# A latent-attention layer on one core: the split of the attention scores goes from fp32r to fp16

## What is computed

```python
q_c = hidden_size @ Wq_c.T + bq_c                               # 192 wide
q = (q_c @ Wq_up.T + bq_up).reshape(b, s, NH, Q_HEAD)            # 128 + 64 per head
kv = hidden_size @ Wkv_c.T + bkv_c                               # 64 + 64 wide
k = concatenate([k_nope, k_rope]); v = ...                       # both from kv
scores = einsum('bhqd,bhkd->bhqk', q, k) / sqrt(Q_HEAD)
attn = softmax(scores, axis=-1)
o = einsum('bhqk,bhkv->bhqv', attn, v)
out = einsum('bhsv,Hv->bsH', o, Wo) + bo                         # heads are summed
```

## Time and profile before

| | |
|---|---|
| median of 3 runs (lowest to highest) | 1978.44 us (1977.9 to 1979.36) |
| the profiled execution, its own time | 1978.39 us |
| its span (first to last instruction) | 1976.4 us |
| mean granted TensorE clock | 0.992 of full speed |
| prepare, attention, feed_forward and what surrounds it | 0 to 93, 93 to 1830, 1830 to 1976 us of the span |
| busy share of the span: PE, PEld, DVE, ACT, POOL | 98%, 73%, 82%, 68%, 56% |

### The profile page before, as it was taken

The page is one execution under the profiler, slowest core; times in us unless marked ns, Lnnn a source line. Parts: engine busy times, 40 slices in busy tenths (PEclk is TensorE's granted clock), DMA queues, the critical chain, the costliest instruction groups (busy, mean ns, idle before and its releaser), DMA issues. The chain is left out here.

```text
span 1976.4 us, 37173 instructions
## 1 busy us (share of the span) xinstructions
PE 1937.1 (98%) x11014; PEld 1441.7 (73%) x11014; DVE 1622.0 (82%) x2585; ACT 1353.8 (68%) x2488; POOL 1102.3 (56%) x1215
## 2 busy tenths in 40 slices
PE   7999999999999999999999999999999999999798
PEld 6767777777777777777777777777777777777576
DVE  6588888888888888888888888888888888888665
ACT  4367777777777777777777777777777777777443
POOL 3336566565665665655656656656656566565710
PEclk9899999999999999999999999999999999999899
DMA  5521111111111111111111111111111111111211
GB/s 201 194 62 32 43 40 34 43 34 41 44 33 43 40 35 43 36 39 43 34 42 43 32 43 40 35 43 36 40 43 32 43 39 35 43 34 33 75 43 43
DMA packets 74308, 95.19 MB, mean 48 GB/s; under 512 B 25856, under 2 KB 48416, under 8 KB 74272
## 3 DMA queue, kind: packets, MB, share of 16 engines
q1 hardware_dynamic: 70176, 86.33, 17.1%
q0 software_dynamic: 4096, 8.40, 1.2%
HBM read 83.95 MB, written 10.75 MB: 48 GB/s over the span
## 5 line engine op out<-in xcount | busy, mean ns | idle before, releaser
L832 DVE TENSOR_TENSOR PTL<-X,PTH 128x512 f16<-128x512 f32 x1024 | 658.6, 685 | 147.8 <-ACT PTH L783 142.0
L783 ACT ACTIVATE PTH<-X 128x512 f16<-128x512 f32 x1024 | 554.3, 594 | 281.5 <-PE X L692 281.5
L848 DVE TENSOR_REDUCE mx<-S 128x1 f32<-128x1024 f32 x512 | 623.6, 1218 | 3.0 <-PE S L712 3.0
L798 ACT ACTIVATE prob<-S,shift 128x1024 f32<-128x1024 f32 x512 | 574.2, 1121 | 1.7 <-DVE shift L856 1.6
L692 PEld LDWEIGHTS X<-ident,prob 128*128 128x128 f32 x4096 | 469.2, 141 | 120.6 <-issue 53.3
L692 PE MATMUL X<-ident,prob 128*128 128x128 f32 x4096 | 538.1, 274 | 5.3 <-ACT prob L798 5.3
L710 PE MATMUL S<-kvTH,qeH 128*128 128x512 f32 x1024 | 445.5, 435 | 1.6 <-DVE qeL L837 1.6
L712 PE MATMUL S<-kvTH,qeL 128*128 128x512 f32 x1024 | 406.0, 396 | 0.0
L711 PE MATMUL S<-kvTL,qeH 128*128 128x512 f32 x1024 | 401.9, 392 | 0.0
L658 POOL TENSOR_TENSOR onormH<-osum,recip_row 128x512 fp32r<-128x512 f32 x128 | 198.5, 1551 | 288.7 <-ACT osum L806 288.7
L643 POOL TENSOR_TENSOR wvH<-wv,unit_tile 128x128 fp32r<-128x128 f32 x128 | 57.4, 448 | 393.4 <-PE V L763 387.7
(11 more groups left out here) (202 smaller groups left out, 1972.2 us busy)
## 6 DMA issues: line engine op xcount, KB each, us to landing
recip_row<-row_scratch SPq DMA_DIRECT2D x128, 256.0 KB, 4.2
weff<-weff_scratch SPq DMA_DIRECT2D x128, 192.0 KB, 4.0
wv<-in_wv POOLq DMA_DIRECT2D x128, 64.0 KB, 3.7
raw<-in_raw SPq DMA_DIRECT2D x8, 772.0 KB, 5.2
weff_scratch<-w_split SPq DMA_DIRECT2D x8, 768.0 KB, 4.8
x<-in_x SPq DMA_DIRECT2D x4, 1024.0 KB, 6.8
x_all<-in_x SPq DMA_DIRECT2D x3, 1024.0 KB, 6.8
out<-y SPq DMA_DIRECT2D x3, 1024.0 KB, 4.2
```

The source lines that it names most:

```text
L783: nc.scalar.activation(PTH[p][:, part:part + 4, unit * P:(unit + 1) * P], X[:, k % 2, :].rearrange("p (k c) -> p k c", k=4), ACT.Copy).the ...
L798: nc.scalar.activation(prob[u][:], S[:, u % 2, :], ACT.Exp, bias=shift[:, col:col + 1], accum_out=rs[:, col:col + 1]).then_inc(probs_ready, 1)
L832: v.tensor_tensor(PTL[p][at], X[:, k % 2, :].rearrange("p (k c) -> p k c", k=4), PTH[p][at], ALU.subtract).then_inc(low_out, 1)
L848: v.reduce_max(mx[:, col:col + 1], S[:, u % 2, :], AX.X).then_inc(max_ready, 1)
```

## The change

The scores are computed from fp16 halves in place of fp32r ones. fp16 has a narrow range of exponents, so both sides are scaled by powers of two: the key latents by `scale` (per latent, from the bound that also scales the values) while ACT reads them, and the projected queries by `qscale`, from a bound on what a query can reach; the exponential multiplies the scores by `unscale`.

In attention: kvTH, kvTL, qeH, qeL are fp16. ACT reads O twice, to qef (fp32) and to qeH (fp16), each with bias and scale tiles; POOL subtracts them to qeL at the end of its step, and DVE's `low_q` is gone. PE waits for q_high, not q_low, before it uses O again. The exponential takes a scale tile. DVE makes the shift with two dependent instructions on 128x1, not one.

In prepare: DVE takes two maxima of absolute values per group of heads; ACT takes absolute values of all latent weights, not of the key ones alone; PE adds eight one-column matmuls in the last turn and three small ones near the end, two of which wait for DVE's steps; DVE adds `reach_of_queries` ahead of wcAH and `scale_of_queries` in place of one instruction (L484). The matmul with `diag` becomes a transpose.

The diff, without declarations of tiles and semaphores and the renamed lines of the key bound:

```diff
             def turn_back(n):
 
-                pe.wait_ge(diag_ready, 1)
                 for u in range(UN):
-                    last = mm(psN[:, u * KVL:(u + 1) * KVL], kvf[0:KVL, u * P:(u + 1) * P], diag[:], start=True, stop=True)
+                    last = nc.tensor.transpose(psN[:, u * KVL:(u + 1) * KVL], kvf[0:KVL, u * P:(u + 1) * P], ident[0:KVL, 0:KVL])
                 last.then_inc(n_done, 1)
 
             def turn(n, nxt):
                 if nxt is None:
                     project(n, (0,))
+                    pe.wait_ge(wabs_ready, 3)
+                    for c in (1, 2):
+                        for k in range(KT):
+                            last = mm(psT[0][:, c - 1:c], wabs[:, k, c * P:(c + 1) * P], ones[:], start=(k == 0),
+                                      stop=(k == KT - 1))
+                    last.then_inc(qbound_done, 1)
...
                 mm(out, wcBHL[:], keep["qbL"][:, tok], start=False, stop=True).then_inc(cT_done, 1)
+                if n == 1:
+                    pe.wait_ge(q_step, REACH)
+                    pe.wait_ge(n_out, NB + 1)
+                    mm(psN[:, B0 + 1:B0 + 2], ones_all[:], reach[:, 0:1], start=True, stop=True).then_inc(reach_done, 1)
+                if n == 2:
+                    pe.wait_ge(q_step, TERM)
+                    pe.wait_ge(proj_out, 3 * NB)
+                    mm(psB[0:1, 0:P], term[:], ident[:], start=True, stop=True).then_inc(term_turned, 1)
+            pe.wait_ge(q_step, TOP)
+            mm(psN[:, B0 + 2:B0 + 3], ones_all[0:1, :], top[0:1, :], start=True, stop=True).then_inc(top_spread, 1)
...
-                for half in range(2):
-                    nc.scalar.activation(wabs[:, :, half * KVL:(half + 1) * KVL], wl[:, :, 0:KVL],
-                                         ACT.Abs).then_inc(wabs_ready, 1)
-                nc.scalar.activation(pbabs[:], pb[:, 3:4], ACT.Abs).then_inc(wabs_ready, 1)
+                nc.scalar.activation(wabs[:, :, 0:P], wl[:, :, 0:P], ACT.Abs).then_inc(wabs_ready, 1)
+                nc.scalar.activation(pbabs[:], pb[:], ACT.Abs).then_inc(wabs_ready, 1)
                 read_turned(n, range(UN))
+                nc.scalar.activation(wabs[:, :, P:3 * P], wl[:, :, P:3 * P], ACT.Abs).then_inc(wabs_ready, 1)
...
+                    if j == 0:
+                        act.wait_ge(k_scaled, 1)
+                    factor, bias = (scale[:, 0:1], kbias[:, 0:1]) if j == 0 else (1.0, pb[:, j:j + 1])
+                    nc.scalar.activation(out[:], src[:], ACT.Identity, bias=bias, scale=factor)
+                    nc.scalar.activation(keep[hi][:, tok], src[:], ACT.Identity, bias=bias, scale=factor).then_inc(proj_out, 1)
...
                 high, low = split[i][:, :, 0, :], split[i][:, :, 1, :]
+                v.reduce_max(wmax[:, ds(g, 1), 0], full[:, :, 0, :], AX.XY, apply_absolute_value=True)
+                v.reduce_max(wmax[0:QB, ds(g, 1), 1], full[0:QB, :, 1, :], AX.XY, apply_absolute_value=True)
...
                 dve.wait_ge(scale_out, 1)
                 v.tensor_scalar(scale[:], scale[:], 2.0 ** 14, None, ALU.mult).then_inc(scale_out, 1)
                 dve.wait_ge(scale_out, 2)
-                v.tensor_scalar(diag[:], ident[0:KVL, 0:KVL], scale[0:KVL, 0:1], None, ALU.mult).then_inc(diag_ready, 1)
+                v.tensor_scalar(kbias[:], pb[:, 0:1], scale[:, 0:1], None, ALU.mult).then_inc(k_scaled, 1)
+
+            def reach_of_queries():
+
+                dve.wait_ge(qbound_done, 1)
+                v.scalar_tensor_tensor(out=bound[:, 1:3], in0=psT[0][:, 0:2], scalar=NORM_MAX, in1=pbabs[:, 1:3],
+                                       op0=ALU.mult, op1=ALU.add).then_inc(q_step, 1)
+                dve.wait_ge(split_done, groups + 1)
+                v.reduce_max(wtop[:], wmax[:].rearrange("p g s -> p s g"), AX.X).then_inc(q_step, 1)
+                dve.wait_ge(q_step, 2)
+                v.tensor_tensor(reach[:, 1:2], wtop[:, 1:2], bound[:, 2:3], ALU.mult).then_inc(scale_out, 1)
+                dve.wait_ge(scale_out, 3)
+                v.scalar_tensor_tensor(out=reach[:, 0:1], in0=wtop[:, 0:1], scalar=bound[:, 1:2], in1=reach[:, 1:2],
+                                       op0=ALU.mult, op1=ALU.add).then_inc(q_step, 1)
+
+            def scale_of_queries():
+
+
+                dve.wait_ge(bias_in, 16)
+                v.tensor_scalar(keep["beff"][KVL:P, :], bqr[KVL:P, :], SCALE, None, ALU.mult).then_inc(q_step, 1)
+                dve.wait_ge(q_step, 4)
+                v.reduce_max(btop[:], keep["beff"][:], AX.X, apply_absolute_value=True).then_inc(q_step, 1)
+                dve.wait_ge(q_step, 5)
+                dve.wait_ge(reach_done, 1)
+                v.scalar_tensor_tensor(out=term[:], in0=psN[:, B0 + 1:B0 + 2], scalar=btop[:, 0:1], in1=kinv[:],
+                                       op0=ALU.add, op1=ALU.mult).then_inc(q_step, 1)
+                dve.wait_ge(term_turned, 1)
+                v.reduce_max(top[0:1, :], psB[0:1, 0:P], AX.X).then_inc(q_step, 1)
+                dve.wait_ge(top_spread, 1)
+                v.tensor_scalar(qpower[:], psN[:, B0 + 2:B0 + 3], TINY, None, ALU.max).then_inc(q_step, 1)
+                dve.wait_ge(q_step, 8)
+                v.tensor_scalar(qpower[:].bitcast(I32), qpower[:].bitcast(I32), 0x7F800000, None,
+                                ALU.bitwise_and).then_inc(q_step, 1)
+                dve.wait_ge(q_step, 9)
+                v.tensor_scalar(keep["unscale"][:], qpower[:], 2.0 ** -14, None, ALU.mult).then_inc(q_step, 1)
+                dve.wait_ge(q_step, 10)
+                v.reciprocal(qpower[:], keep["unscale"][:]).then_inc(q_step, 1)
+                dve.wait_ge(q_step, 11)
+                v.tensor_tensor(keep["qscale"][:], qpower[:], kinv[:], ALU.mult).then_inc(q_step, 1)
+                dve.wait_ge(q_step, 12)
+                v.tensor_scalar(keep["beff"][:], keep["beff"][:], keep["qscale"][:, 0:1], None, ALU.mult)
...
+                    reach_of_queries()
...
-        qeH = [sb(f"qeH{i}", [P, BLK], F32R) for i in range(2)]
-        qeL = [sb(f"qeL{i}", [P, BLK], F32R) for i in range(2)]
+        qef = [sb(f"qef{i}", [P, BLK]) for i in range(2)]
+        qeH = [sb(f"qeH{i}", [P, BLK], F16) for i in range(2)]
+        qeL = [sb(f"qeL{i}", [P, BLK], F16) for i in range(2)]
...
+
+            def low_q(nxt, i):
+                pool.wait_ge(q_high, nxt + 1)
+                nc.gpsimd.tensor_tensor(qeL[i][:], qef[i][:], qeH[i][:], ALU.subtract).then_inc(q_low, 1)
+
+            low_q(0, 0)
...
+                if exists(g) and exists(g + 1):
+                    if not isinstance(g, int) or g >= 1:
+                        pool.wait_ge(wv_split, g)
+                    low_q(g + 1, 1 - par)
...
                         if exists(g + 1) and on:
-                            pe.wait_ge(q_low, g + 2)
+                            pe.wait_ge(q_high, g + 2)
...
-                nc.scalar.activation(qeH[i][:], O[:], ACT.Identity, bias=keep["beff"][:, ds(h, 1)]).then_inc(q_high, 1)
+                bias, factor = keep["beff"][:, ds(h, 1)], keep["qscale"][:, 0:1]
+                nc.scalar.activation(qef[i][:], O[:], ACT.Identity, bias=bias, scale=factor)
+                nc.scalar.activation(qeH[i][:], O[:], ACT.Identity, bias=bias, scale=factor).then_inc(q_high, 1)
...
                     nc.scalar.activation(prob[u][:], S[:, u % 2, :], ACT.Exp, bias=shift[:, col:col + 1],
+                                         scale=keep["unscale"][:, 0:1],
...
-            def low_q(nxt, h, i):
-                dve.wait_ge(q_high, nxt + 1)
-                v.scalar_tensor_tensor(out=qeL[i][:], in0=O[:], scalar=keep["beff"][:, ds(h, 1)],
-                                       in1=f32(qeH[i][:]), op0=ALU.add, op1=ALU.subtract).then_inc(q_low, 1)
-
-            low_q(0, 0, 0)
...
-                    v.scalar_tensor_tensor(out=shift[:, col:col + 1], in0=mx[:, col:col + 1], scalar=bias, in1=lifted,
-                                           op0=ALU.add, op1=ALU.subtract, reverse1=True).then_inc(shift_ready, 1)
+                    v.scalar_tensor_tensor(out=top[:, col:col + 1], in0=mx[:, col:col + 1], scalar=keep["unscale"][:, 0:1],
+                                           in1=bias, op0=ALU.mult, op1=ALU.add).then_inc(top_ready, 1)
+                    dve.wait_ge(top_ready, 4 * g + u + 1)
+                    v.tensor_tensor(shift[:, col:col + 1], lifted, top[:, col:col + 1], ALU.subtract).then_inc(shift_ready, 1)
...
-                    if u == 1 and on and exists(g + 1):
-                        low_q(g + 1, h + 1 if not isinstance(g, int) else (h + 1) % NH, 1 - par)
...
-                "inv": sb(inner, "kv_inv", [P, 1]),
-                "kvTH": sb(inner, "kvTH", [P, TOK], F32R), "kvTL": sb(inner, "kvTL", [P, TOK], F32R),
+                "inv": sb(inner, "kv_inv", [P, 1]), "qscale": sb(inner, "q_scale", [P, 1]), "unscale": sb(inner, "unscale", [P, 1]),
```

(26 more changed lines are left out.)

38 lines of the change are left out of this document (21 added, 17 removed).

## The result

The changed kernel takes **2120.62 us** (median of four runs, 2107.1 to 2128.01) against 1978.47 in the same comparison: a ratio of **1.071** (95% interval 1.0655 to 1.0765). Forecast were 2040 us and a range of 1998 to 2058, so the direction was right and the size was not: +142 in place of +62. The profiled execution took 2118.55 us (span 2116.9). The four runs lie 1% apart, those of the kernel before 0.07%.

What follows compares the result with a forecast made beforehand. ACT's serial stretch before the transposes was to bound each head, outweighing PE's fp16 saving: 1978.4 + 49.5 (attention) + 11 (preparation) + 1.3 (first head) = 2040 us, 3.1% slower, range 1998 to 2058, chance 0.63.

Steps and rivals of the forecast that it cites:

- What bounds a head: Attention: ACT's serial stretch before the probability transposes grows 0.86 us, so a head takes 13.96 us against 13.57.
- PE's printed wait: Before L692's transposes, PE was to show idle time put down to ACT's exponential, about 90 us in all.
- The second pointer operand: Scale tile beside the bias or shift tile in ACT's query reads and exponential: 0.09 us charged for each.
- Rival A: ACT's activations: the second tile operand is free, stretch grows 0.59, +0.12 us per head, 2005 us; chance 0.18.
- fp16 matmuls: PE's 24 score matmuls per head start 0.014 to 0.015 us closer, saving 0.36 us per head.
- C: PE's score matmuls: fp16 runs no faster than fp32r, +0.66 us per head, 2075 us; chance 0.05.
- B: Attention: ACT's stretch doesn't set the transposes' start, PE's saving stays, head 13.21 us, total 1945 us; chance 0.11.
- The failed step: DVE's longer shift before the exponential: covered by ACT's copies and query reads, priced at nothing; uncovered 0.3 us per unit.
- the sign: Named as showing the forecast wrong: a wait for DVE's shift in front of an engine; no size given.
- Preparation: Before attention: added maxima, matmuls, hops and small ops cost 11 us, between 4 and 15.
- The maxima: Preparation, DVE's two per group of heads: 1.4, 2 and 2.4 us in the loop's turns, 1.4 in the last.
- one-column matmuls, hops and small ops: Preparation's last turn and end: matmuls 1.8 us, four dependent small ops of 0.2, hops with end ops 1.

Runs made afterwards that it cites:

- shift_one_tensor: Changed kernel, with the shift's two small DVE instructions each reading one SBUF tensor and taking other values as pointer scalars: 2036.26 us, ratio 1.0288.
- fp16_alone: Kernel before, with only kvTH, kvTL, qeH and qeL turned to fp16, no scaling: 1928.33 us, ratio 0.9748.
- act_alone: Kernel before in fp32r, with only the second ACT read of O and a scale tile of ones at all three activations: 2066.02 us, ratio 1.0445.
- one_step_two_tensors: Changed kernel, with the shift made by one DVE instruction with two SBUF tensors, c left out: 2040.22 us, ratio 1.0311.

## Why the prediction was right and wrong, point by point

- **What bounds a head: right.** ACT's serial stretch in front of the transposes was the place. Where nothing is held a head is 13.93 us against 13.96. PE's printed wait was forecast too high: it is 58.4 us in `shift_one_tensor`, against some 90; in the changed kernel the holds brought it to 122.6. `fp16_alone` and `act_alone` came to 13.17 and 14.21 against 13.21 and 14.23.
- **The second pointer operand: right**, by the step of the first: 687 to 780, 1121 to 1214. The Trainium skill's 93 ns ("ScalarE: Activation LUTs", section "What ACT_TABLE_LOAD costs") agrees with both. Rival A falls.
- **fp16 matmuls: right.** In the long head above scores start at 686.60, 686.82, 687.03, 687.25, 687.47 and 687.68, 0.216 apart. C falls. B falls for the changed kernel, whose ACT stretch grew by 0.84 us (3.60 in `shift_one_tensor`, 1009.12 to 1012.72, against 2.76), but its time of a head is what `fp16_alone` shows.
- **The failed step**: "The longer shift of units 1 to 3 lands in the time in which ACT copies two PTH tiles (1.08 us), and of unit 0 in the query reads, so I price it at nothing; uncovered it would be 0.3 per unit." The cover was there; the price was not 0.3. I took the mean of L856 (278 ns) as what such an instruction costs, and a mean hid two kinds. The view of L856 alone shows it, in the kernel before:

```profile
L856 DVE SCALAR_TENSOR_TENSOR shift<-mx,c_all,c_lift x512: 218/221/1600, 100.3 to 1837.9; 128x1 f32<-128x1 f32 x171
```

  A median of 221 and a longest of 1600 ns for 128 elements. Some were held already: 128 of the 512 last over 0.3 us, 117 of them (0.41 us, as a rule) ending together with POOL's L643. Two in series meet POOL's products (1.5 us each) far more often, cost up to 1.57 + 1.36 us in place of 0.38, and 1.08 us of cover doesn't hide that. It is 79 us of the 142, nearly all of the miss of 81. I had named the sign ("a wait for DVE's shift ... in front of an engine instead") but gave it no case and no price, so my range ended at 2058. The rival that was missing needed POOL's timeline beside DVE's, which I read only for its busy time and its queue.
- **Preparation: too small by what this execution shows.** 14.6 us to the first read against 11, within my 4 to 15. But up to 6.9 of the 14.6 are not the change's own work: with the same preparation the first read came at 102.3 in `one_step_two_tensors` and at 109.2 in `shift_one_tensor`, by the clock and the early hold shown above. The maxima (8.5 against 7.2 charged) and the rest (6.1 against 3.8) are therefore not told apart with certainty. What the one-column matmuls, hops and small ops cost was not tried.
- **The sum as measured**: 14.6 to the first read + 45.2 for the longer stretch less PE's saving + 79.4 for the holds + 1.4 behind the last read = 140.6, the difference of the spans (2116.9 - 1976.4 = 140.5). Without the holds it is 61.2, where 61.8 was forecast (49.5 + 11 + 1.3). That it is so close is partly luck: attention came 4.3 us cheaper than forecast, the rest 3.7 dearer, and the rest moves by several us between kernels with the same preparation.

## What to carry to other kernels

Look at the shortest, median and longest duration of a tiny instruction, not its mean: where the longest is as long as another engine's instruction, put the two timelines side by side. On DVE, write small arithmetic that stands in front of another engine with one tensor input and pointer operands (`tensor_scalar`), when GpSimd works on SBUF at the same time. The runs show this for 128x1; a `tensor_scalar` over 128x512 was held (3.65 us, above). And before adding a read to the engine with the serial stretch, ask which engine has that time free at that point of its own queue.
